# Low-part value matmuls in one run at the end of a tile, and the query projections moved from bank 1 to bank 3

## The reference

```
q = (x @ Wq).reshape(h, n, d)        # a reshape: head i is rows i*256 .. i*256+255 of x @ Wq
k = (x @ Wk).reshape(h, n, d); v = (x @ Wv).reshape(h, n, d)
a = einsum('hnd,hmd->hnm', q, k) * d ** -0.5
a = a + adj + adj
a = where(adj == 0, -1000000.0, a)
a = softmax(a, axis=-1)
a = where(adj == 0, 0.0, a)
out = einsum('hnm,hmd->hnd', a, v).transpose(1, 0, 2).reshape(n, h * d) @ Wout
result = layernorm(x + out)          # over the last axis, eps 1e-5
```

## Time and profile before

| | us |
|---|---|
| median of 3 runs | 1822.61 |
| lowest, highest | 1822.05, 1825.81 |
| the profiled execution | 1825.55 |
| its span, first to last instruction | 1823.8 |
| TensorE busy | 1794.9 |
| VectorE, GpSimd, ScalarE busy | 1112.3, 983.8, 854.3 |

### The profile page before, as it was taken

One profiled execution on the slowest core, in us unless ns is written; L12 is line 12 of the kernel. 1 busy time (PEld: TensorE's weight loads), 2 busy tenths in 40 slices (PEclk: granted clock), 3 DMA queues, 4 the chain that ended last, 5 costly groups with the idle time before them and its releaser, 6 DMA issues.

```text
span 1823.8 us, 29365 instructions
## 1 busy us (share of the span) xinstructions
PE 1794.9 (98%) x10272; PEld 1582.9 (87%) x10272; DVE 1112.3 (61%) x2318; ACT 854.3 (47%) x1411; POOL 983.8 (54%) x762
## 2 busy tenths in 40 slices
PE   8999889999999999999999999999999999999998
PEld 7987779888998889988899888988889888898887
DVE  6888855555555655556554555555555556546667
ACT  5655454444454445444454444544445444544433
POOL 6888764544644555444554555644455455554443
PEclk9999999999999999999999999999999999999999
DMA  7888875666656666466665666656655566655664
GB/s 251 246 255 269 249 215 155 191 193 195 174 160 184 192 195 188 141 198 195 189 188 144 199 188 191 182 156 201 192 177 175 162 199 197 185 160 172 175 174 139
DMA packets 186995, 345.97 MB, mean 190 GB/s; under 512 B 39392, under 2 KB 96736, under 8 KB 170464
## 3 DMA queue, kind: packets, MB, share of 16 engines
q10 hardware_dynamic: 92032, 200.59, 35.2%
q1 hardware_dynamic: 94816, 143.50, 28.7%
HBM read 190.84 MB, written 18.87 MB: 115 GB/s over the span
## 4 chain that ended last, share of the span: by engine, by line
PE 85%; SPq 2%; DVE 2%; DMA 1%; issue 1%; POOL 0%; ACT 0%; ACTq 0%; DVEq 0%
PE bank L401 33%; PE y_bank L417 22%; PE bank L366 18%; PE y_bank L425 12%; SPq L305 2%; DMA p_turned<-blocks 1%; DVE blocks L666 1%; POOL p_split L483 0%; DVE y_acc L754 0%; ACTq L579 0%; PE bank L386 0%; ACT m_sb L570 0%; DVE zero_mark L702 0%; DVE small L673 0%; DVE t_p L643 0%
## 5 line engine op out<-in xcount | busy, mean ns | idle before, releaser
L483 POOL TENSOR_TENSOR p_split<-p_turned,p_split 128x512 fp32r<-128x512 f32 x510 | 649.7, 1302 | 563.1 <-ACT p_split L551 562.8
L401 PE MATMUL bank<-k_split,q_split 128*128 128x512 f32 x3072 | 789.3, 392 | 2.0 <-DVE small L643 2.0
L401 PEld LDWEIGHTS bank<-k_split,q_split 128*128 128x128 f32 x3072 | 557.2, 189 | 104.4 <-DVE small L643 3.3
L417 PE MATMUL y_bank<-v_split,p_split 128*128 128x512 f32 x2048 | 547.2, 390 | 2.4 <-ACT p_split L551 2.4
L643 DVE CUSTOM_DVE_ANT_0 t_p<-bank,m_sb 128x512 f32<-128x512 f32 x512 | 351.6, 687 | 207.2 <-PE bank L401 178.6
L417 PEld LDWEIGHTS y_bank<-v_split,p_split 128*128 128x128 f32 x2048 | 384.3, 188 | 84.5 <-ACT p_split L551 3.7
L542 ACT ACTIVATE t_p<-t_p,small 128x2048 f32<-128x2048 f32 x128 | 257.3, 2010 | 353.7 <-DVE small L655 349.4
L472 POOL TENSOR_TENSOR w_slot<-raw_w,w_slot 128x512 fp32r<-128x512 f32 x192 | 249.6, 1301 | 233.8 <-ACT w_slot L522 230.6
L551 ACT ACTIVATE p_split<-p_turned 128x512 fp32r<-128x512 f32 x512 | 288.8, 621 | 113.3 <-DMA p_turned<-blocks 109.0
L666 DVE STREAM_TRANSPOSE blocks<-t_p 128x2048 f32<-128x2048 f32 x128 | 295.8, 2311 | 61.2 <-ACT t_p L542 45.3
L366 PE MATMUL bank<-x_t,w_slot 128*128 128x256 f32 x2304 | 307.8, 285 | 11.9 <-issue 7.8
(11 more groups left out here) (44 smaller groups left out, 634.8 us busy)
## 6 DMA issues: line engine op xcount, KB each, us to landing
m_sb<-m_dram ACTq DMA_DIRECT2D x112, 1024.0 KB, 5.3
p_turned<-blocks SPq DMA_DIRECT2D x1532, 64.0 KB, 2.2
p_turned<-blocks ACTq DMA_DIRECT2D x516, 64.0 KB, 2.7
blocks<-in_adj_dram SPq DMA_DIRECT2D x64, 256.0 KB, 4.0
raw_w<-in_L_gnn_Wv_dram ACTq DMA_DIRECT2D x64, 256.0 KB, 3.5
m_dram<-m_sb SPq DMA_DIRECT2D x16, 1024.0 KB, 6.5
raw_w<-in_L_gnn_Wq_dram ACTq DMA_DIRECT2D x63, 256.0 KB, 3.4
raw_w<-in_L_gnn_Wk_dram ACTq DMA_DIRECT2D x61, 256.0 KB, 3.9
```

Of the source, the lines that this page charges most:

```text
L401: mm = nc.tensor.matmul(dst[:], q[:, a, k, f * P:(f + 1) * P], k_split[:, kk, k, b * BANK:(b + 1) * BANK], start=(i == 0), stop=(i == len( ...
L417: nc.tensor.matmul(y[:], p_split[tau % 2][:, HI, j * P:(j + 1) * P], v_split[:, j].rearrange("p s d -> p (s d)"), start=(j == 0), stop=False)
L483: nc.gpsimd.tensor_tensor(lo, p_turned[:, i * BANK:(i + 1) * BANK].rearrange("p (j b) -> p j b", b=QUAD), hi.bitcast(F32), ALU.subtract).t ...
```

## The change

Two numbers. `LO_EVERY` goes from 2 to 4, and the query pieces of the even tiles 0 to 12 are due at bank 3 instead of bank 1 (except in the very first step, where bank 2 stays). The first query piece of the next head stays at bank 2 of tile 14. Since `due` also sets the ring and the order of the weight blocks, these follow.

```diff
-LO_EVERY = 2
+LO_EVERY = 4
...
-            if t % 2 == 0 and t <= LAST_Q and b == (2 if tau == 0 else 1):
+            if t % 2 == 0 and t <= LAST_Q and b == (2 if tau == 0 else 3):
                 yield "q", h, t // 2 + 1
```

## The result

The changed kernel took 1834.26 us, median of six runs (1829.08 to 1837.07), against 1824.09 for six runs of the kernel before (1822.05 to 1825.81). The ratio is 1.005 (95% interval 1.0041 to 1.006), some 9 us slower by that ratio (the medians themselves differ by 10.2). I had forecast 1824.6 and given 0.63 to no difference; the time lies above my range. Of the distance to 1824.6, 1.5 us is the base and not the change: I had added to 1822.61, the median of three runs, and six give 1824.09. Its profiled execution took 1829.08 us (span 1827.3) and is the shortest of the six, so this trace holds only part of the loss. I profiled the same kernel three times for that reason. The comparison that closes is +3.5 us against the profiled execution before.

The account below looks back on a forecast made before the run. TensorE's matmul spacings bound heads 1 to 7, VectorE's chain up to tile 14 bounds head 0. Terms -1.8 + 3.7 + 0 + 0.1 = +2.0 us on 1822.61 gave 1824.6, range 1820.0 to 1828.8.

Parts of the forecast that it names:

- part 3: Heads 1 to 7, later queries: high parts shift by up to 2 us, covered by 8 us before TensorE's values; 0.
- Weight splits on ScalarE and GpSimd: Heads 1 to 7: these splits move with the query and are due two keys ahead; 0.
- Rival C: Heads 1 to 7, tiles 11 to 12: SyncE's x load makes a stall outlasting its cover, 1 us a head; 1831.6; chance 0.06.
- part 1: Heads 1 to 7: one run of sixteen saves 90 narrow stretches at 0.02 us, 1.8 us gained; head 0 nothing.
- Part 2: Head 0, even tiles 2 to 12: q's low part behind the row maximum delays VectorE, 3.7 us lost in sum.
- The six waits for shuffles: Head 0: six transposes waited for shuffles, 5.7 us in all; even ones absorb delay in tiles 6, 10 and partly 12.
- the projection of 234.80: End of head 0: it and tile 14's row maximum should come 3 to 4 us later, through VectorE's chain.
- Part 4: Tail: the last query shifts tile 124's transpose by about 1.2 us, mostly hidden; 0.1 us lost.

Follow-up runs that it names:

- e1: Changed kernel with the query pieces back at bank 1, so only LO_EVERY = 4 remains: 1826.89 us, ratio 1.0005 to the kernel before.
- e2: Changed kernel with LO_EVERY back at 2, so only the queries at bank 3 remain: 1828.19 us, ratio 1.0014 to the kernel before.
- e5: Changed kernel with two runs of eight again in the steps of tiles 2, 3 and 15: 1826.61 us, ratio 1.0016 to the kernel before.
- e6: Changed kernel with runs of eight in tiles 2, 3, 15 and the x load behind the fourth shuffle piece: 1824.29 us, ratio 0.9997.
- e7: Changed kernel with queries at bank 1 and two runs of eight in tiles 0, 2, 3 and 15: 1822.78 us, ratio 0.9988.
- e10: Changed kernel with runs of eight in tiles 0, 2, 3, 15, x load behind the fourth shuffle piece, head 0 queries at bank 1: 1821.68 us, ratio 0.9982.
- e8: Changed kernel with only the last query piece of each head (tile 12) back at bank 1: 1827.96 us, ratio 1.0019 to the kernel before.
- e9: Changed kernel with queries at bank 1 except each head's last one (tile 12), which stays at bank 3: 1833.98 us, ratio 1.0042.
- e4: Kernel before, with SyncE's x load also waiting until the values of tile 12's step are done: 1824.39 us, ratio 0.9996.
- e3: Changed kernel with SyncE's x load behind the fourth shuffle piece instead of the second: 1825.56 us, ratio 1.0001 to the kernel before.

## Why the prediction was wrong

**The step that failed is part 3, "this covers it: 0".** It had three faults.

First, the consumer. I asked who waits for the high parts of p and found only TensorE's values three steps later, with 8 us of cover. They did stay covered. But ScalarE and GpSimd are in order, and behind the late high and low parts of p in tile 15 stood the high and low parts of the key pieces' weights, with no slack. "Weight splits on ScalarE and GpSimd ... are due two keys ahead: 0" was said of a move of under 2 us; the last high part of tile 59 ended 6.1 us later, and tile 61's was still 3.8 late (907.15 against 903.37).

Second, the size. I put the shift at up to 2 us. SyncE's hold was 4.3 us, and the mask tile beside the loads it released took 10.2 us where it had taken 6.0. Rival C had the place (the x load that holds SyncE, tiles 11 and 12) and the price of 1 us a head (1831.6 us; the measured time is 2.7 above that), but named the wrong consumer, and I gave it 0.06 because of the 8 us.

Third, part 1 and part 3 were priced apart. Eight narrow matmuls moved from bank 1 to bank 3 are no work less, but between two pieces they are 0.95 us in which VectorE and GpSimd catch up. I counted the low parts of p that these matmuls need, and not the pieces that no longer have them as a cushion. e1, e2 and the pair put the joint part at 5.6 us, give or take 3; e5 returns 6.2.

**Part 1 was right for heads 1 to 7.** Plain tiles are 0.02 us shorter, and e6 gives 1.8 us there. The spacings here are 120 and 227 ns. The Trainium skill (TensorE: Matmul & The Clock Gate, Back-to-back issue gap) gives columns over the clock plus 2.5 ns for an isolated matmul, by my estimate from it 109 and 216, with no term for what stands beside, and warns that a stream is spaced otherwise; by that formula the merging would have given nothing, and the trace disagrees.

**Part 2: the mechanism was right in tiles 4 and 8, the sum was not seen.** VectorE of the changed kernel in tile 8 answers to the earlier trace rows:

```profile
145.82 0.16 DVE L655 TENSOR_REDUCE small<-small 128x1 f32<-128x5 f32 x1 [0.23 <-DVE small L643]
...
146.90 0.69 DVE L626 SCALAR_TENSOR_TENSOR q_split<-bank,q_split 128x512 fp32r<-128x512 f32 x1 [0.92 <-ACT q_split L536]
...
150.37 2.30 DVE L666 STREAM_TRANSPOSE blocks<-t_p 128x2048 f32<-128x2048 f32 x1
```

The low part stands behind the row maximum and waited 0.92, where I had said 0.5 to 0.8. From one transpose to the next, tile 4 went from 12.84 to 13.78 and tile 8 from 12.83 to 13.96: 0.9 and 1.1, for my 1.2. Tile 6 took 14.10 for 14.02 and tile 10 13.81 for 14.62: absorbed, as said, and tile 10 more than that. What I left out is the tiles between. The six waits for shuffles went to none:

```profile
DVE zero_mark L702 <- ACT m_sb L570: 8.0, 24, 0.3
DVE q_split L626 <- ACT q_split L536: 4.2, 5, 1.0
```

A transpose that comes later waits less in the next tile, so I should have summed pairs of tiles and not even tiles. In this execution head 0 ended 0.24 us earlier, not 3.7 later: the row maximum of tile 14 came at 226.61 against 227.84, the projection of 234.80 at 233.58, and already tile 2's transpose, where I had put 0.7 us of loss, came 0.73 earlier (70.66 against 71.39).

That is not the cost of the late queries alone. The start of tile 16 in the profiles, one execution each, sorts like this (e7 and e10 keep runs of eight in some tiles; e8 at 248.14 and e9 at 248.23 mix early and late queries): with runs of eight and early queries 249.11 (before) and 248.72 (e4), with runs of eight and late queries 250.53 (e2); with runs of sixteen and early queries 246.57 to 247.65 (e1, e7, e10), with runs of sixteen and late queries 248.30 to 250.30 (the changed kernel three times, e3, e5, e6). By these means the late queries cost 1.6 to 2.4 us in head 0, and the run of sixteen gave back about as much, where I had written that in head 0 it is "worth nothing". The medians point the same way: e10 with early queries in head 0 stands 2.8 us below e6 with late ones, with intervals of ±1.6 each and a tile 0 that differs too, and e7 gained 2.2 us, of which the spacings in heads 1 to 7 are 1.0. With so few executions this is an estimate and not shown; why the run of sixteen should help in head 0 is open.

**Part 4** can't be told from none: from the start of tile 127 to the end it took 35.96 us before and 35.92, 36.00 and 36.02 in the three profiles of the changed kernel.

The rest of the size, 9.1 us against 3.8 in the first profile, is the spread of the collision: the third profile shows 13.8 of the same kinds in the same places. What differs is how late tile 13's high parts come; why they come later in one execution than in another I can't say.

## What to carry to other kernels

When a result comes later, list everything that is queued behind the instruction that waits for it, on each in-order engine, and ask of each when it is due; the slack of the result's own consumer says nothing of the others. Work that is moved away from between two dependent pieces is cover that is lost, although no work was added, so price it with the delays that other parts of the change bring. Where a held queue releases its loads together with others, look at what starts in that microsecond: putting one load behind six that were ready gave back 9 us.

## What the runs showed of the hardware

**A one-column operation on VectorE took up to six times as long.** Its line in the changed kernel (shortest, median, longest in ns, first to last us):

```profile
L673 DVE SCALAR_TENSOR_TENSOR small<-small x128: 214/217/1390, 41.2 to 1805.3; 128x1 f32<-128x1 f32 x128
```

36 of 128 took over 250 ns (32 before, 45 in the third profile, 84 to 89 in e1, e7 and e9), and each of these ends within 25 ns of the end of a GpSimd operation with two tensor inputs. Here that is GpSimd's:

```profile
533.05 1.30 POOL L472 TENSOR_TENSOR w_slot<-raw_w,w_slot 128x512 fp32r<-128x512 f32 x1
```

532.97 + 1.39 and 533.05 + 1.30 end within 0.01 us. The Trainium skill (SBUF — State Buffer, SBUF: two separate sides) has VectorE and GpSimd share a pair of ports under an exclusive lock, which would fit. What makes the difference is how much of GpSimd's operation is left. In the kernel before, none of the 96 short ones began with more than 0.18 us of one left (0.23 over all profiles), and 25 of the 32 long ones began with 0.38 to 1.14 us left and ended with it. The other 7 began, as 85 short ones did, within the last tenths of a us of one GpSimd operation with the next about to start, and were held for the whole of that next one; tile 3's are of this kind. Which of these are held and which slip through is open.

**Loads issued within a microsecond of each other landed later, but not all of them.** The 1 MB mask tile took 4.9 us in e4, 6.0 before and 10.2 in the changed kernel; over the six heads it took 4.9 to 5.4, 5.3 to 6.0 and 8.0 to 10.2. The six 64 KB shuffles behind the x load took 4.1 to 4.7 us in e4 and 4.0 to 4.7 before (medians of each head), 5.9 to 6.4 in the changed kernel, and 2.0 to 2.7 in e3, where they go ahead of it. The 256 KB x load went the other way: 5.5 to 6.1, 4.6 to 5.3 and 3.4 to 3.6. The core moved 214, 239 and 215 GB/s in the stretches shown (changed, before, e4).

**One kernel, one order of instructions, 1829 to 1841 us.** The kernel before spread over 6.6 us (1822.00 to 1828.63), the changed one over 11.5 (1829.08 to 1840.61), with stalls at fixed places in a varying number of heads. One profile of it showed a third of the loss.
